# Pairs of token tiles multiplied by the folded matrix in seven half-size products

## The reference, cut to what matters

```python
x = x + L0_ffn(L0_cond(x, W[condition]))      # per-sample 64x64 mixing, router over 256 slots, gate
x = x + L1_ffn(L1_cond(x, adapter_ids))       # base weight + bias + a rank-16 adapter per sample,
                                              # then W_base, a low-rank Fourier update, bias
```

## Time and profile before

| | us |
|---|---|
| median of 3 runs (lowest, highest) | 1557.77 (1557.37, 1563.2) |
| the profiled execution | 1556.96 |
| its span, first to last instruction | 1555.1 |
| PE busy | 1505.8 (97%) |
| DVE, ACT, POOL busy | 867.4, 790.0, 354.7 |
| mean granted TensorE clock | 0.994 of full speed |

### The profile page before, as it was taken

One profiled execution on the slowest core, in us unless ns is written; L12 is line 12 of the kernel. 1 busy time (PEld: TensorE's weight loads), 2 busy tenths in 40 slices (PEclk: granted clock), 3 DMA queues, 4 the chain that ended last, 5 costly groups with the idle time before them and its releaser, 6 DMA issues.

```text
span 1555.1 us, 27462 instructions
## 1 busy us (share of the span) xinstructions
PE 1505.8 (97%) x7676; PEld 940.8 (60%) x7676; DVE 867.4 (56%) x2598; ACT 790.0 (51%) x1675; POOL 354.7 (23%) x212
## 2 busy tenths in 40 slices
PE   5897999989999999999999999999999999999998
PEld 3676777655555555555555555655555656555554
DVE  5664777775555555555555555555555555555554
ACT  4575666644444444444444444444444444444443
POOL 4664666311111111111111111111111111111110
PEclk9998999999999999999999999999999999999999
DMA  9586556253233333333333333333232222333321
GB/s 300 194 292 217 179 187 186 71 135 90 91 91 89 89 90 92 91 90 91 93 94 97 90 90 92 97 95 90 89 89 89 89 89 89 89 89 89 90 74 53
DMA packets 160937, 175.98 MB, mean 113 GB/s; under 512 B 104851, under 2 KB 123238, under 8 KB 160785
## 3 DMA queue, kind: packets, MB, share of 16 engines
q1 hardware_dynamic: 156118, 161.56, 34.5%
q10 hardware_dynamic: 4795, 14.15, 2.7%
HBM read 135.97 MB, written 39.32 MB: 113 GB/s over the span
## 4 chain that ended last, share of the span: by engine, by line
PE 82%; POOL 7%; issue 6%; DVE 3%; DMA 1%; ACT 1%; SPq 1%; ACTq 0%; POOLq 0%; DVEq 0%
PE pair L1384 42%; PE pair L86 7%; PE pair L87 7%; POOL v_lo L246 7%; PE pair L88 7%; PE pair L1346 7%; PE pair L1354 6%; PE pair L1320 2%; PE pair L1406 1%; PE pair L1405 1%; PE pair L1413 1%; DMA v_x<-in_x 1%; PE pair L1335 1%; DVE m_lo L1440 1%; PE pair L1325 0%
## 5 line engine op out<-in xcount | busy, mean ns | idle before, releaser
L1384 PE MATMUL pair<-m_hi,t_x_hi 128*128 128x512 f16 x1024 | 306.4, 381 | 1.1 <-DVE m_lo L1440 1.1
L1384 PE MATMUL pair<-m_hi,t_x_lo 128*128 128x512 f16 x1024 | 305.0, 379 | 0.0
L1384 PE MATMUL pair<-m_lo,t_x_hi 128*128 128x512 f16 x1024 | 305.0, 379 | 0.0
L1221 POOL TENSOR_TENSOR t_narrow<-t_a_raw,t_narrow 128x256 f16<-128x256 f32 x64 | 43.9, 686 | 1046.7 <-ACT t_x_hi L1108 1046.7
L246 POOL TENSOR_TENSOR v_lo<-v_x,v_hi 128x1024 fp32r<-128x1024 f32 x64 | 154.8, 2421 | 101.0 <-ACT v_hi L240 100.6
L1384 PEld LDWEIGHTS pair<-m_hi,t_x_lo 128*128 128x128 f16 x1024 | 100.3, 98 | 121.2 <-issue 0.6
L1384 PEld LDWEIGHTS pair<-m_lo,t_x_hi 128*128 128x128 f16 x1024 | 100.2, 98 | 121.1 <-issue 0.6
L86 PE MATMUL pair<-t_narrow,t_x_hi 128*128 128x352 f16 x512 | 160.1, 313 | 0.1
L87 PE MATMUL pair<-t_narrow,t_x_hi 128*128 128x352 f16 x512 | 160.2, 313 | 0.0
L88 PE MATMUL pair<-t_narrow,t_x_lo 128*128 128x352 f16 x512 | 160.0, 313 | 0.0
L1175 ACT COPY t_out_sb<-pair 128x1024 f32<-128x1024 f32 x64 | 64.9, 1014 | 169.4 <-PE pair L1354 169.4
(11 more groups left out here) (252 smaller groups left out, 2838.0 us busy)
## 6 DMA issues: line engine op xcount, KB each, us to landing
v_x<-in_x SPq DMA_DIRECT2D x64, 512.0 KB, 3.6
t_xt<-in_x_t SPq DMA_DIRECT2D x64, 512.0 KB, 3.2
out<-t_out_sb SPq DMA_DIRECT2D x64, 512.0 KB, 2.7
t_rhs_b<-bk_hi SPq DMA_DIRECT2D x256, 64.0 KB, 2.3
t_a_raw<-in_lora_a SPq DMA_DIRECT2D x128, 64.0 KB, 2.8
t_bd<-w_kinds SPq DMA_DIRECT2D x128, 64.0 KB, 2.3
t_rhs_c<-bk_lo SPq DMA_DIRECT2D x128, 64.0 KB, 2.2
blk_raw<-in_left_blocks ACTq DMA_DIRECT2D x10, 512.0 KB, 4.3
```

The source lines that it names most:

```text
L1384: last = pe.matmul(pm_ps[:, c], lhs, m[:, k, c], start=a, stop=z)
```

## The change

Tiles are taken in pairs (n-1, n), n odd. With the pair as two block rows and M as 2x2 blocks of 512x512, the product is made by Strassen's scheme in the form with seven products and shared sums. Four of the seven right factors are sums of blocks of M (`t_sums`, made once by POOL); four of the left ones are sums of halves of x (`sums`, made by POOL in place in the two slots of `xt`, with their own high and low halves, `sums_high` on ACT and `sums_low` on POOL). A product is four units of three matmuls of 512 columns, so 84 for a pair, not 96. They share the two banks of `pm_ps`: B11 and, onto it, B21, and T2, then T3 in the odd step; the rest of T3, T1, T4 and, onto T1, B22 in the even step. DVE adds the parts in SBUF (`p1`, `u2`, `u3`, `c22`), and from these the high parts (ACT) and low parts (DVE) of the four quarters are made; the last quarter (first tile of the pair, right half) is made at the start of the next odd step. The output stage of a tile runs three steps after its step, the loop is unrolled four times, and steps 64 to 66 drain it. Tiles of x and of the adapter's columns are loaded two at a time in the SP queue's odd steps and split two steps ahead. The scale of all split operands is halved. Several tiles share memory that was separate before.

```diff
@@ SP, a step
+        def step(n, q):
+            p = q % 2
+            if not isinstance(n, int) or n < NT:
+                load_conditions(n, q)
+                load_wa(n, p)
+            if not isinstance(n, int) or n - 2 < NT:
+                load_adapters(n - 2, p)
+            store(n - 4, p)
+            if p and (not isinstance(n, int) or n + 2 < NT):
+                load_x(n + 1, 0)
+                load_x(n + 2, 1)
@@ ACT, a step
+            if last_quarter(n, q):
+                act.wait_ge(s["sums_done"], n * 3 - 3)
+                act.copy(col[0:1, 14:15], g["ones"][0:1, 0:1])
+                act.activation(pm_hi[0][:, RIGHT], u2[:], ACT.Identity, scale=unscale(n - 3)
+                               ).then_inc(s["c_hi_ready"], 1)
...
+            if p == 0 and (not isinstance(n, int) or 0 < n < NT):
+                sums_high(n, q)
...
+            if first_part(n, q):
+                act.wait_ge(s["prod_done"], n * 4 - 3)
+                act.copy(p1[:], pm_ps[:, LEFT]).then_inc(s["p1_ready"], 2)
             if has_new(n):
                 act.wait_ge(s["arg_ready"], n + 1)
                 act.activation(b["th"][:], b["arg"][:], ACT.Tanh, scale=TANH_C
                                ).then_inc(s["tanh_ready"], 1)
+            if p == 1 and (not isinstance(n, int) or 1 < n < NT - 2):
+                split_x(n + 2, (q + 2) % 4)
...
+            if first_part(n, q):
+                act.wait_ge(s["prod_done"], n * 4 - 1)
+                act.activation(pm_hi[0][:, LEFT], pm_ps[:, LEFT], ACT.Identity, scale=unscale(n - 1)
+                               ).then_inc(s["c_hi_ready"], 1)
+            if second_part(n, q):
+                act.wait_ge(s["sums_done"], n * 3 - 2)
+                act.activation(pm_hi[1][:, RIGHT], c22[:], ACT.Identity, scale=unscale(n - 1)
+                               ).then_inc(s["c_hi_ready"], 1)
...
                 act.copy(b["e_t"][:].rearrange("p c n -> p (c n)"), misc_ps[:, P:3 * P]
                          ).then_inc(s["et_ready"], 1)
+            if second_part(n, q):
+                act.wait_ge(s["sums_done"], n * 3 - 1)
+                act.copy(col[0:1, 14:15], g["ones"][0:1, 0:1])
+                act.activation(pm_hi[1][:, LEFT], u3[:], ACT.Identity, scale=unscale(n - 1)
+                               ).then_inc(s["c_hi_ready"], 1)
...
+            elif p == 0 and (not isinstance(n, int) or n + 2 < NT):
+                split_x(n + 2, (q + 2) % 4)
@@ POOL, a step
+        def sums(n):
+            a1, a2, c1_, c2 = (b["xt"][:, slot, cols] for slot in range(2) for cols in (LEFT, RIGHT))
...
+            pool.tensor_tensor(c2, c1_, c2, ALU.add).then_inc(s["s_sums"], 1)
+            pool.wait_ge(s["s_sums"], done + 1)
+            pool.tensor_tensor(c1_, a1, c1_, ALU.subtract).then_inc(s["s_sums"], 1)
+            pool.wait_ge(s["s_sums"], done + 2)
+            pool.tensor_tensor(a1, c2, a1, ALU.subtract).then_inc(s["s_sums"], 1)
+            pool.wait_ge(s["s_sums"], done + 3)
+            pool.tensor_tensor(a2, a2, a1, ALU.subtract).then_inc(s["s_sums"], 1)
...
+        def step(n, q):
+            new = not isinstance(n, int) or n + 2 < NT
+            if q % 2 == 0 and (not isinstance(n, int) or 0 < n < NT):
+                sums_low(n, q)
...
+            if new and (not isinstance(n, int) or n > 0):
+                split_x(n + 2, (q + 2) % 4)
+            if q % 2 == 1 and new:
+                sums(n + 1)
@@ PE, a step
+                if k == (5 if one else 2):
+                    aux(n)
+                if k == (7 if one else 6):
+                    aux_t(n)
             if has_old(n):
+                if p:
+                    pe.wait_ge(s["c_lo_ready"], n * 2 - 2)
...
+            units = product_first(n, q) if p else product_second(n, q)
...
+                if done == 2:
+                    query_t(n)
+                if done == 6:
+                    scores(n)
+                if done == 13:
+                    probs_t(n)
@@ DVE, a step
+            if last_quarter(n, q):
+                dve.wait_ge(s["prod_done"], n * 4 - 4)
+                dve.tensor_tensor(u2[:], pm_ps[:, LEFT], u2[:], ALU.add).then_inc(s["sums_done"], 1)
...
+            if last_quarter(n, q):
+                dve.wait_ge(s["c_hi_ready"], n * 2 - 2)
+                low_part(n - 3, 0, RIGHT, u2[:]).then_inc(s["c_lo_ready"], 2)
...
+            if first_part(n, q):
+                dve.wait_ge(s["prod_done"], n * 4 - 2)
+                dve.wait_ge(s["p1_ready"], n + 1)
+                dve.tensor_tensor(u2[:], pm_ps[:, RIGHT], p1[:], ALU.add).then_inc(s["sums_done"], 1)
```

More of the change, by code:

```diff
@@ L955, in main_stage @@
     BPT = 16 * 2
[L956 removed]
+    WPT = 16 * 2
+    LPT = 16 * 6
     def sync(sp):
@@ L1052, in sync @@
         sp.wait_ge(s["wa_stored"], 16)
+        load_wa(0, 0)
+        load_wa(1, 1)
+        load_x(2, 0)
+        load_x(3, 1)
         sp.wait_ge(s["vb_ready"], 1)
@@ L1057, in sync @@
         load_adapters(1, 1)
[L1058 to L1072, removed]
+        for q in (2, 3):
+            sp.wait_ge(s["mixq_done"], q - 1)
+            load_conditions(q, q)
+            load_wa(q, q % 2)
+        load_x(4, 0)
+        load_x(5, 1)
+        def step(n, q):
[9 more added lines that the diff above has]
+                load_x(n + 2, 1)
+        with sp.Fori(0, NT // 4 - 2) as j:
+            for q in range(4):
+                step(j * 4 + (4 + q), q)
+        for n in range(NT - 4, NT + 4):
+            step(n, n % 4)
         for p in range(2):
@@ new lines, in sums_low @@
+        def sums_low(n, q):
+            for slot, count in ((1, 1), (0, 2)):
+                pool.wait_ge(s["s_hi_ready"], n + count)
+                pool.tensor_tensor(s16[q // 2][1][:, slot, :], b["xt"][:, slot, :], s16[q // 2][0][:, slot, :],
+                                   ALU.subtract).then_inc(s["s_lo_ready"], 1)
+        split_x(0, 0)
+        pool.wait_ge(s["v_mm_ready"], 1)
+        t_sums(T1)
+        split_x(1, 1)
+        t_sums(T2)
+        sums(0)
+        sums_low(0, 0)
+        t_sums(T3)
@@ L1296, in tensor, with aux, aux_t @@
         pe.wait_ge(s["wu_split"], 2)
         pe.wait_ge(s["cleared"], 1)
-        def step(n, p):
-            o = 1 - p
+        def aux(n):
+            pe.wait_ge(s["et_ready"], n)
+            for c in range(2):
+                last = pe.matmul(misc_ps[:, 3 * P:3 * P + BOT], b["e_t"][:, c, :], g["vd"][:, c, :],
+                                 start=(c == 0), stop=(c == 1))
+            last.then_inc(s["u_done"], 1)
+        def aux_t(n):
+            pe.wait_ge(s["u_split"], n * 2)
+            pe.transpose(misc_ps[:, 0:P], f(b["u_sb"][:]), g["ident"][:]).then_inc(s["ut_done"], 1)
@@ L1301, in step @@
+        def step(n, q):
+            p = q % 2
+            o, oq = 1 - p, (q - 3) % 4
+            start, one = isinstance(n, int) and n == 0, isinstance(n, int) and n == 1
             if has_new(n):
@@ L1417, in step @@
-                if not has_old(n):
-                    pe.wait_ge(s["vd_ready"], 1)
+            if one:
+                adapter(n, q)
+            if start:
+                pe.wait_ge(s["lsum1_ready"], 1)
+                pe.wait_ge(s["router_split"], 2)
+                pe.matmul(score_ps[:, 0:1], g["ones"][:], b["mean"][:, 0:1], start=True, stop=True
+                          ).then_inc(s["mean_done"], 1)
+                value_operand(0, range(KC // 2))
+                query_t(0)
+                value_operand(0, range(KC // 2, KC))
+                scores(0)
+                value_operand(1, range(KC))
+                return
@@ L1420, in tensor @@
+            units = product_first(n, q) if p else product_second(n, q)
+            if not (first_part(n, q) or second_part(n, q)):
+                return
+            for done, _ in enumerate(units, start=1):
+                if not has_new(n):
+                    continue
+                if done == 2:
[4 more added lines that the diff above has]
+                    probs_t(n)
         steps(pe, step)
@@ L1590, in step @@
                                   ).then_inc(s["z_ready"], 1)
-                if not has_old(n):
-                    beside_first()
+            if start:
+                variance_norm()
+                for u in range(2, 6):
+                    m_low(u)
+            if one:
+                m_low(10)
+                m_low(11)
+            if has_new(n):
                 dve.wait_ge(s["z2_ready"], n + 1)
```

647 lines of the change are left out of this document (406 added, 241 removed).

## The result

The changed kernel takes 1836.84 us (median of 4 runs, 1834.33 to 1839.05); the kernel before, beside it, 1557.96. The ratio is 1.178, 95% interval 1.1762 to 1.1797: slower by 279 us. The forecast was 1820, with a range of 1600 to 1900.

What follows compares the result with a forecast made beforehand. PE bounds the kernel before; after the change, other queues stall it in odd steps. Head 378 plus 30 pairs of 46.4 plus 49 of tail gave 1819 of span; forecast 1820 us, 8-in-10 range 1600 to 1900.

Steps and rivals of the forecast that it cites:

- What bounds it: Mid run before: PE busy in all of 500 us at full clock; after, whether the other queues let PE run.
- PE stays the bound: Rival: PE stays the bound, only faster, with waits under 2.1 us a pair; 1497 us, chance 0.09 for below 1549.
- The gain: Products with M: 12 fewer matmuls a pair at 0.215, 2.58 us; a pair without waits 35.6.
- First chain: Odd step: late x load, ACT's split, pm_hi and DVE's low part beside POOL hold PE's output stage; stall 7.6, pair 43.2.
- E: The end of the even step's output stage on PE, from which the forecast counted the odd step's links.
- Second chain: Gate in the odd step: dot product behind POOL's subtraction delays e_t and SCALE; 1.5 us a pair, bounds 0 and 3.4.
- The clock: PE's granted clock falls to half after the odd-step stall; 1.6 us a pair, bounds 0 and 2.2.
- The pair: Two steps in mid run, with stall, gate and clock: 46.4 us.
- The tail: From step 63's start through steps 64 to 66, copy and store: 49 us.
- The head: Up to step 3's start, with POOL's 35 us of splits and sums before step 2: 378, give or take 10.
- Only ACT's order counts: Rival: only ACT's order makes PE wait, 2.3 to 5 us a pair; 1566 to 1640 us, chance 0.13.
- One of load and port fails to bite: Rival: no waits for POOL gives 1728 us, x in time gives 1690; from 1640 to 1760, together 0.22.

Runs made afterwards that it cites:

- run 7: Changed kernel with the three POOL and ACT moves of run 2, run 4 and run 6 together: 1536.36 us, ratio 0.9861 to the kernel before.
- run 1: Changed kernel, SP issues both tiles of x of an odd step ahead of conditions, wa and adapters: 1745.92 us, ratio 1.1203 to the kernel before.
- run 3: Changed kernel, POOL's low part of the even tile waits for DVE's low part of the last quarter: 1757.82 us, ratio 1.1279 to the kernel before.
- run 2: Changed kernel, ACT's split of the even tile moved into the odd step behind the last quarter's pm_hi and pa_hi: 1628.96 us, ratio 1.0452.
- run 5: Changed kernel with the edits of run 2 and run 4 together: 1566.78 us, ratio 1.0056 to the kernel before.
- run 6: Changed kernel, in odd steps POOL's split of the odd tile waits for DVE's dot product: 1799.11 us, ratio 1.1545 to the kernel before.
- run 9: run 7 plus conditions of tiles 2 and 3 loaded ahead of SP's wait for the fold's vb: 1529.24 us, ratio 0.9814 to the kernel before.
- run 11: run 9 plus, in step 1, ACT's split of tile 2 moved behind the tanh: 1524.77 us, ratio 0.9792 to the kernel before.
- run 4: Changed kernel, in even steps POOL's low parts of the sums wait for DVE's operations on hm: 1843.68 us, ratio 1.1818 to the kernel before.

## Why the prediction was right, and where it was not

**What bounds it.** Right. The rival in which PE stays the bound needed waits under 2.1 us a pair; they came to 4.82 + 1.87 + 0.83 = 7.5, and the clock on top.

**The gain.** Right, shown by run 7: 35.68 against a forecast of 35.6 for a pair without waits.

**First chain.** Right in each link. From E to the odd output stage: forecast 21.9, measured 1206.68 - 1185.03 = 21.65, and 21.20 in the next pair. The load is issued at E + 11.4 (forecast 11.5), ACT has `pm_hi` at E + 18.9 (19.4), the low part ends at E + 21.6 (21.9). The 7.6 us of stall were forecast in one piece, though; PE lost 1.87 of them at `query_t` already, which the forecast had put under the same cover, and stood still for 4.82 before the output stage. Each link was then taken out by itself: load 3.04 a pair (run 1), port, that is DVE held back by POOL, 2.67 (run 3), split 6.94 (run 2), each with its share of the clock. They don't add up: 3.04 and 2.67 are inside the 6.94, since the split's move takes load and port off the chain too.

**Second chain.** Right in kind, sized 1.5, which is too high: 36.78 - 35.68 = 1.10 at full clock with the other waits gone (run 5 to 7); the 1.37 of run 6 alone has some clock in it. Its parts were a little off: `SCALE` was expected to wait for one of POOL's half sums, with `u_sb` as late as `e_t`; in the trace only `e_t` shows as a wait.

**The clock.** Forecast 1.6 a pair, bounds 0 and 2.2; measured 1.9 (5.44 - 3.52 on the odd output stage). From the output stage to the next E the pair shown took 1230.55 - 1206.68 = 23.87, the one before it 25.1, the mean from 600 to 1400 us 24.34; the forecast had 21.3 + 1.5 + 1.6 = 24.4. That the sum fits so well is partly luck: the gate is 0.4 too high and the clock 0.3 too low.

**The pair** was forecast 46.4 and measured, from step 3's first product to step 63's, (1791.31 - 420.20)/30 = 45.70. That is 21 us less over 30 pairs, most of it in the first chain, which took 21.4 in the mean (45.75 - 24.34) and not 21.9. The tail from there is 1837.2 - 1791.3 = 45.9, not 49.

**The head is the step that was off.** Forecast: step 3 at 378, give or take 10. Measured, in PE's timeline of the kernel after (first products of steps 2 and 3, and the wait between them):

```profile
385.78 0.48 PE L86 MATMUL pair<-t_narrow,x_hi 128*128 128x352 f16 x1 [5.77 <-POOL x_lo L1364]
...
407.98 0.63 PE L86 MATMUL pair<-t_pa_hi,t_bd 128*128 128x320 f32 x1 [9.87 <-DMA t_bd<-w_kinds]
...
420.20 0.31 PE L86 MATMUL pair<-t_narrow,x_hi 128*128 128x352 f16 x1
```

42 us late. I had added up POOL's work (35 us) and let PE follow. From step 0's first product (319.66) to step 3's PE needs 100.5 us, where the kernel before needs 63.9 (315.64 to 379.57), and its waits there sum to 40.4 us, against 4.2 before. So waits fill nearly the whole difference of 36.6, and the forecast had none among them but POOL's. Another 4.0 lie ahead of step 0, whose start varies from 314.5 to 319.7 between the profiled versions of the changed kernel. The conditions of tile 2, 9.9, are queued in SP behind a wait for the fold (run 9: 7.1 us). ACT's splits of tiles 2 and 3 stand behind the whole gate of step 1, which makes the 5.8 for POOL's low part (run 11 moves one; 1.6 us of it reach step 3). The others, 7.9 for `vd` ahead of step 1, 4.8 for `pa_lo`, 4.0 for `u_sb` and 3.9 for the query, no run takes out. And PE, busy in 62 of 105 us there, has a granted clock of 0.69 in place of 0.98; what that costs, and what POOL's block sums cost, was not tried. In run 7, with PE the bound in mid run, the account against the kernel before is this: 30 pairs save 30 x (38.19 - 35.68) = 75; step 3 begins at 417.82, not 379.57, which takes 38 of them; and the tail from step 63, 45.9 instead of 29.9, takes 16. The 21 that are left are the difference of the two profiled spans, 1555.1 - 1534.1.

**The sum.** 1819 of span against 1837.2: +42 for the head, -21 for the pairs, -3 for the tail. The total is closer than its parts deserve; two errors half cancel. The range did not depend on that.

**Rivals.** "Only ACT's order counts" said that with x in time the stall left would be 2.3 a pair. Run 1 shows 2.90, with the port in it: its low part still takes 2.53 where 0.75 is its own. Without the port some 1.1 would be left, by estimate (2.90 - 1.78), so that rival's 2.3 was too high; no run takes load and port out together. "One of load and port fails to bite" is refuted by runs 1 and 3 in the kernel as it stands.

## What to carry to other kernels

Removing work from the bound engine pays only if the engines that feed it keep up in *order*, not in amount: here 12 matmuls less a pair were worth 2.5 us, and one `split_x` that stood ahead of one `pm_hi` in ACT's queue cost 6.9. When an edit that removes a visible wait brings nothing, look where the wait has gone before dropping it: the same line brought 0 us while another chain set the end, and 62 once that chain was cut. And a wait on TensorE has a second price: behind one of 2 to 3 us the clock cost 0 or 1.5 us more here, behind one of 4.5 to 5 us 1.3 to 2.7.

## What the runs showed of the hardware

**The exclusion of DVE and POOL depends on the operands, not the size.** In run 6 a gate operation of one column with two SBUF operands meets POOL's subtraction (timeline, POOL and DVE):

```profile
1194.35 2.13 POOL L1366 TENSOR_TENSOR x_lo<-t_xt,x_hi 128x1024 f16<-128x1024 f32 x1
...
1195.03 0.75 DVE L1812 SCALAR_TENSOR_TENSOR t_pm_lo<-pair,t_unscale,t_pm_hi 128x512 fp32r<-128x512 f32 x1
...
1195.70 0.14 DVE L1937 TENSOR_SCALAR t_col<-t_col 128x1 f32<-128x1 f32 x1
1195.88 0.63 DVE L1939 SCALAR_TENSOR_TENSOR t_col<-t_col 128x1 f32<-128x1 f32 x1
```

It takes 0.63 in place of 0.16 and ends at 1196.51, with POOL's end at 1196.48, while the one-column operation with one operand (0.14) and the 128x512 low part that takes its first operand from PSUM (0.75) pass through the same subtraction unhindered. The casts of `hm`, though, have a single SBUF operand and take 1.91 and 2.05 us beside POOL's subtractions; with POOL held back (run 4) each takes 0.22. The Trainium skill ("SBUF — State Buffer", Who interferes with whom) states both: two SBUF inputs contend, and casts can in a two-port mode. By that rule, the trace agrees. I had read from it that the gate operations would be hit like the long ones; of these only the ones with two SBUF inputs are, and in the kernel after they mostly fell between two of POOL's half sums (0.18).

**The clock does not fall after each wait of one length.** Behind equal waits of 2.90 it fell in every second pair of run 1. In run 6 it fell behind 2.07 as well; in the kernel after it did not behind 1.87. What decides between a fall and none was not tried.
